# Twelve of thirty-two loop sums as three 16-bit products, and the projection moved ahead of the messages

## The reference

```python
h = x @ W_loop.T
g = h @ Wg_loop.T
vals = (h + b_loop) * sigmoid(g + bg_loop)
x1 = layernorm(x + relu(adj.T @ vals))          # first layer, per graph
out = layernorm(x1 + (adj @ x1) @ weight[0] + bias)   # second layer, per graph
```

## Time and profile before

| | |
|---|---|
| median of 3 runs | 158.79 us (158.68 to 159.75) |
| the profiled execution | 159.41 us, of which its span is 157.7 us |
| TensorE busy in that span | 148.8 us (94%) |
| VectorE, ScalarE, GpSimd busy | 124.1, 122.8, 125.7 us (79%, 78%, 80%) |
| mean granted TensorE clock | 0.987 of full speed |

### The profile page before, as it was taken

One profiled execution on the slowest core, in us unless ns is written; L12 is line 12 of the kernel. 1 busy time (PEld: TensorE's weight loads), 2 busy tenths in 40 slices (PEclk: granted clock), 3 DMA queues, 4 the chain that ended last, 5 costly groups with the idle time before them and its releaser, 6 DMA issues.

```text
span 157.7 us, 3520 instructions
## 1 busy us (share of the span) xinstructions
PE 148.8 (94%) x1040; PEld 136.7 (87%) x1040; DVE 124.1 (79%) x325; ACT 122.8 (78%) x255; POOL 125.7 (80%) x195
## 2 busy tenths in 40 slices
PE   7999999999999999999999999999999999999910
PEld 3688999999999999999999999999999999999800
DVE  1359988888988888887988888887888878989980
ACT  3357876979797997979797997979797997769850
POOL 0606698797979799797979799797979799797970
PEclk9999999999999999999999999999999999999995
DMA  4899999989797988979797989989693929211053
GB/s 126 292 405 394 370 389 404 390 265 389 198 382 230 331 303 258 354 241 398 177 392 209 356 290 286 340 237 373 192 393 130 381 92 303 86 69 69 4 201 138
DMA packets 19606, 42.73 MB, mean 271 GB/s; under 512 B 2177, under 2 KB 3073, under 8 KB 19585
## 3 DMA queue, kind: packets, MB, share of 16 engines
q1 hardware_dynamic: 14544, 25.76, 48.6%
q0 software_dynamic: 4752, 16.52, 30.3%
q10 hardware_dynamic: 288, 0.20, 0.4%
HBM read 34.08 MB, written 8.39 MB: 269 GB/s over the span
## 4 chain that ended last, share of the span: by engine, by line
POOL 65%; PE 15%; issue 13%; DVE 1%; POOLq 1%; ACT 0%; DVEq 0%
POOL rstd L339 31%; POOL x L353 26%; PE hg_ps L423 7%; POOL adj_sb L326 4%; POOL adjt_sb L333 3%; PE loop_ps L439 2%; PE msg_ps L458 2%; PE msg_ps L413 1%; PE y_ps L497 1%; PE hg_ps L407 1%; POOL rstd L363 1%; POOLq L59 1%; DVE s_sb L808 0%; ACT gate L607 0%; POOLq L234 0%
## 5 line engine op out<-in xcount | busy, mean ns | idle before, releaser
L339 POOL TENSOR_TENSOR rstd<-var,power 128x8 f32<-128x8 f32 (+1 forms) x36 | 53.8, 1496 | 18.5 <-DVE var L787 18.4
L423 PE MATMUL hg_ps<-w_all,xt_sb 128*128 128x256 f32 x256 | 65.7, 382 | 0.0
L353 POOL TENSOR_SCALAR x<-s_sb,mean_neg,rstd 128x128 f32<-128x128 f32 x120 | 52.2, 448 | 3.4
L423 PEld LDWEIGHTS hg_ps<-w_all,xt_sb 128*128 128x128 f32 x256 | 44.6, 193 | 4.1 <-issue 0.3
L626 ACT ACTIVATE out_sb<-z_sb,rstd 128x128 f32<-128x128 f32 x120 | 38.1, 390 | 0.4 <-POOL rstd L339 0.4
L800 DVE TENSOR_TENSOR vals<-hg_ps,gate 128x512 f32<-128x512 f32 x32 | 22.1, 690 | 19.3 <-ACT gate L607 19.3
L439 PEld LDWEIGHTS loop_ps<-vals,adj_sb 128*128 128x128 f32 x256 | 33.3, 191 | 1.9 <-issue 0.2
L598 ACT ACTIVATE hg_ps<-gate_b 128x1024 f32<-128x1024 f32 (+1 forms) x32 | 31.8, 998 | 3.2 <-DVE vals L800 2.6
L458 PEld LDWEIGHTS msg_ps<-adjt_sb,x 128*128 128x128 f32 x248 | 31.4, 191 | 3.1 <-issue 1.5
L439 PE MATMUL loop_ps<-vals,adj_sb 128*128 128x128 f32 x256 | 33.8, 275 | 0.1
L458 PE MATMUL msg_ps<-adjt_sb,x 128*128 128x128 f32 x248 | 33.2, 277 | 0.0
(11 more groups left out here) (64 smaller groups left out, 48.2 us busy)
## 6 DMA issues: line engine op xcount, KB each, us to landing
xt_sb<-x_t_dram SPq DMA_DIRECT2D x32, 256.0 KB, 4.9
x_sb<-x_dram SPq DMA_DIRECT2D x32, 256.0 KB, 4.2
out<-out_sb SPq DMA_DIRECT2D x31, 256.0 KB, 4.7
adj_sb<-adj_dram POOLq DMA_DIRECT2D x15, 512.0 KB, 5.2
adjt_sb<-adj_t_dram POOLq DMA_DIRECT2D x15, 512.0 KB, 6.5
adjt_sb<-adj_t_dram POOLq DMA_DIRECT2D x2, 256.0 KB, 6.7
first_edges<-adj_dram SPq DMA_DIRECT2D x1, 256.0 KB, 4.2
adj_sb<-adj_dram POOLq DMA_DIRECT2D x1, 256.0 KB, 6.3
```

What stands on the lines that cost most here:

```text
L339: nc.gpsimd.tensor_tensor(rstd[:, c % RSTD_RING, first:end, :].rearrange("p l b -> p (l b)"), var[:, c % 2, first:end, :].rearrange("p l b ...
L353: done = nc.gpsimd.tensor_scalar(x1[:, q % X1_RING, batch(b)], s_sb[:, q % S_RING, batch(b)], mean_neg[:, c % 2, b:b + 1], rstd[:, c % RST ...
L423: last = nc.tensor.matmul(hg_ps[:, q % 2, b, :], xt_sb[:, q % XT_RING, batch(b)], w_gate, start=False, stop=True, skip_group_check=True)
```

## The change

The loop sums of the groups 5, 7, ... 27 (`SPLIT`, twelve of them) are no longer one fp32 product per graph. VectorE cuts the values into three bf16 parts that add up to the fp32 number: the upper half of the fp32 word as it stands, the upper half of what is left (`below`), and the rest (`lowest`). TensorE multiplies each of the three with the adjacency, which for these groups lies in SBUF as bf16, and adds them up in PSUM. So that a DMA fills a tile of one type, the pairs of groups are loaded as two even groups (fp32) and two odd groups (bf16) from group 4 to group 27 (`unit_of`, `unit_end`).

Beside it: the projection of a group runs in one piece, ahead of the messages; ScalarE computes the gate ahead of the copy of messages; the copy of negated means is gone, and those who read it subtract the mean instead; two of the five bf16 products on the constant tile just ahead of the loop are gone; the next-to-last group is scaled by ScalarE and stored from ScalarE's queue.

```diff
+SPLIT = tuple(range(5, GROUPS - 4, 2))
...
+def unit_of(q):
+    j = q // 4
+    return (2 * j + q % 2, q % 4 // 2) if 4 <= q < GROUPS - 4 else (q // 2, q % 2)
+def unit_end(k):
+    return 4 * (k // 2) + 2 + k % 2 if 2 <= k < PAIRS - 2 else 2 * k + 1
...
             def load_adj(k):
-                    await_count(pool, loop_done, 2 * (k - ADJ_RING) + 2)
-                    pool.dma_start(adj_sb[:, 2 * spot:2 * spot + 2, :].rearrange("p g n -> p (g n)"), adj[k])\
+                        pool.wait_ge(loop_done, unit_end(k - ADJ_RING) + 1)
+                    edges = adj_sb[:, 2 * spot:2 * spot + 2, :]
+                    source = adj[k].rearrange("p (g n) -> p g n", g=2)
+                    if 2 <= k < PAIRS - 2:
+                        if k % 2 == 1:
+                            edges = half_edges(spot)
+                        first = k // 2 * 2
+                        source = adj[first:first + 2, :, k % 2 * W:(k % 2 + 1) * W].rearrange("g p n -> p g n")
+                    pool.dma_start(edges, source).then_inc(adj_in[spot], 16)
...
-            for _ in range(5):
+            for _ in range(3):
                 nc.tensor.matmul(msg_ps[:, :], warm[:, :], warm_wide, start=True, stop=True)
...
             def loop_sum(q):
+                    if q in SPLIT:
+                        pe.wait_ge(split_done, SPLIT.index(q) + 1)
                     for b in range(GB):
+                        if q in SPLIT:
+                            edges = half_edges(unit % ADJ_RING)[:, place, batch(b)]
+                            nc.tensor.matmul(loop_ps[:, batch(b)], edges, upper_half(vals[:, q % 2, batch(b)]),
+                                             start=True, stop=False)
+                            nc.tensor.matmul(loop_ps[:, batch(b)], edges, upper_half(below[:, batch(b)]),
+                                             start=False, stop=False)
+                            last = nc.tensor.matmul(loop_ps[:, batch(b)], edges, lowest[:, batch(b)],
+                                                    start=False, stop=True)
...
-                else:
-                    messages(t - MSG_LAG)
                 project(t, (2, 3))
+                messages(t - MSG_LAG)
...
+                gates(t)
                 copy_messages(t - MSG_LAG)
-                gates(t)
...
+            norm2(GROUPS - 2, every)
+            act.wait_ge(out_done, GROUPS - 1)
+            act.dma_start(out[GROUPS - 2], out_sb[:, (GROUPS - 2) % OUT_RING, :])\
...
+            def split(q):
+                await_count(dve, loop_done, q - 1)
+                dve.wait_ge(vals_done, q + 1)
+                tt(below[:, :], vals[:, q % 2, :], upper_half(vals[:, q % 2, :]), ALU.subtract).then_inc(below_done, 1)
+                dve.wait_ge(below_done, SPLIT.index(q) + 1)
+                tt(lowest[:, :], below[:, :], upper_half(below[:, :]), ALU.subtract).then_inc(split_done, 1)
...
                 values(t)
+                if t in SPLIT:
+                    split(t)
                 first_sum(t - LOOP_LAG)
...
-            last_norm2(LAST - 1, 0, GB, root_count(GROUPS + 2, 1))
```

More of the change, by code:

```diff
@@ L77, in build @@
         vals = sb("vals", [P, 2, W], F32)
+        below = sb("below", [P, W], F32)
+        lowest = sb("lowest", [P, W], BF16)
         s_sb = sb("s_sb", [P, S_RING, W], F32)
@@ L224, in build, with mean_of, upper_half, half_edges @@
         warm_wide = warm[:, None, :].broadcast_to([P, GB, P])
+        def mean_of(c, b):
+            return stats[:, c % STATS_RING, b // 2, 3 * (b % 2) + 1:3 * (b % 2) + 2]
         def batch(b):
             return slice(b * P, (b + 1) * P)
+        def upper_half(tile):
+            return tile.bitcast(BF16).rearrange("p (n two) -> p n two", two=2)[:, :, 1]
+        def half_edges(spot):
+            return adj_sb[:, 2 * spot:2 * spot + 2, :].rearrange("p g n -> p (g n)").bitcast(BF16)\
+                .rearrange("p (g n) -> p g n", g=2)[:, :, 0:W]
         def arrived(q, ring):
@@ L289, in _ @@
                 store(q)
[L290 to L291 removed]
             for p in range(2):
                 span = slice(2 * p * P, 2 * (p + 1) * P)
[L294 removed]
+                sp.wait_ge(out_dve, p + 1)
                 sp.dma_start(out[LAST, :, span], out_sb[:, LAST % OUT_RING, span])\
@@ L354, in norm1 @@
                         x1[:, q % X1_RING, batch(b)], s_sb[:, q % S_RING, batch(b)],
-                        mean_neg[:, c % 2, b:b + 1], rstd[:, c % RSTD_RING, 0, b:b + 1], ALU.add, ALU.mult)
+                        mean_of(c, b), rstd[:, c % RSTD_RING, 0, b:b + 1], ALU.subtract, ALU.mult)
                 done.then_inc(x1_done, 1)
@@ L429, in loop_sum @@
                 if exists(q):
-                    spot = q // 2 % ADJ_RING * 2 + q % 2
+                    unit, place = unit_of(q)
+                    spot = unit % ADJ_RING * 2 + place
                     if q == 0:
@@ L433, in loop_sum @@
                     else:
-                        pe.wait_ge(adj_in[q // 2 % ADJ_RING], arrived(q // 2, ADJ_RING))
+                        pe.wait_ge(adj_in[unit % ADJ_RING], arrived(unit, ADJ_RING))
                     pe.wait_ge(vals_done, q + 1)
+                    if q in SPLIT:
+                        pe.wait_ge(split_done, SPLIT.index(q) + 1)
                     await_count(pe, s_done, q)
                     for b in range(GB):
-                        last = nc.tensor.matmul(loop_ps[:, batch(b)], adj_sb[:, spot, batch(b)],
-                                                vals[:, q % 2, batch(b)], start=True, stop=True)
+                        if q in SPLIT:
[6 more added lines that the diff above has]
+                                                    start=False, stop=True)
+                        else:
+                            last = nc.tensor.matmul(loop_ps[:, batch(b)], adj_sb[:, spot, batch(b)],
+                                                    vals[:, q % 2, batch(b)], start=True, stop=True)
                     last.then_inc(loop_done, 1)
@@ L660, in look @@
                     await_count(act, seen_done, k)
-                    nc.scalar.activation(seen[:, :], adj_sb[:, 2 * spot:2 * spot + 2, :].rearrange("p g n -> p (g n)"),
+                    edges = adj_sb[:, 2 * spot:2 * spot + 2, :]
+                    if 2 <= k < PAIRS - 2 and k % 2 == 1:
+                        edges = half_edges(spot)
+                    nc.scalar.activation(seen[:, :].rearrange("p (g n) -> p g n", g=2), edges,
                                          ACT.Square, bias=half[:, 0:1],
@@ L783, in variances @@
                 both = stats[:, c % STATS_RING, 2 * first:2 * end, :].rearrange("p c (i k) -> p (c i) k", k=3)
-                if first == 0:
-                    await_count(dve, x1_done, c - 2)
-                    ts(mean_neg[:, c % 2, :], both[:, 0:GB, 1], -1.0, None, ALU.mult)
                 ts(var[:, c % 2, first:end, :].rearrange("p l b -> p (l b)"), both[:, :, 2], 1.0 / P, EPS,
```

16 lines of the change are left out of this document (9 added, 7 removed).

## The result

The changed kernel takes 191.49 us (median of 4 runs, 190.77 to 193.79), the kernel before in the same session 159.27 (4 runs): 1.2005 times as long, with a 95% interval of 1.1908 to 1.2102. That is far above the predicted range. The profiled execution has a span of 192.1 us and a granted TensorE clock of 0.989 (before 0.987), so the clock plays no part. It is the longest of the four runs and left out of the ratio; 1.5 us of it is a wait ahead of the first projection, which the other kernels with the same start don't show.

What follows compares the result with a forecast made beforehand. TensorE was taken to set the pace before, the loop through GpSimd and ScalarE after: +1.4 us for the loop, -0.3 start, -0.4 tail, so +0.7 and a median from 158.79 to 159.5 us; range 156.5 to 163.2.

Steps and rivals of the forecast that it cites:

- The copy of means gives back 0.08.: VectorE's time: dropping the copy of negated means saves 0.08 us, part of its 8.80 us per pair of steps.
- GpSimd's norm instructions keep their length: Sign to look for in the changed profile: GpSimd's norm no longer than before, root and norm together 3.41 us.
- 0 to 0.05: TensorE's wait for ScalarE's copy of messages, in steps whose loop sum isn't split and takes 0.90 us.
- 8.73 to 8.93: Microseconds TensorE by itself needs per pair of steps, with split products and the waits for ScalarE's copy.
- The split on TensorE: Loop sum of split groups: twelve bf16 products at 0.056 us each, 0.67 in all, 0.22 us less per pair.
- The rival of slow products: Split products take 0.11 us each, 9.25 us per pair, 163.3 us in all; chance 0.10 together with longer DMA issues.
- 0.13 to 0.28: TensorE's wait in microseconds for ScalarE's copy of messages, in steps whose loop sum is split and takes 0.67.
- The loop: Chain VectorE, GpSimd, ScalarE, message weights decides: 8.91 to 8.99 us per pair, taken as 8.94, +1.4 us over twelve pairs.
- if that doubled: GpSimd's first load issue, 0.59 us, taken at its old price; doubled by smaller pieces, a pair would take 9.24 us.
- Subtractions against GpSimd: Rival: VectorE's two-SBUF-input subtractions and GpSimd's norm block each other, loop +0.43 to 0.86 us, 162.1 to 164.7 us; chance 0.20.
- Late adjacency: Rival: odd groups' adjacency lands too late for the loop sum, 0.3 us per pair, +3.6, 163.1 us; chance 0.05.
- The ends: Start with two products fewer, -0.3 us (0 to -0.6); tail with the store on ScalarE's queue, -0.4 (-1.1 to +0.3).

Runs made afterwards that it cites:

- e2: Kernel before, with GpSimd's norm subtracting the mean read from the statistics instead of adding the negated copy: 189.72 us, ratio 1.1924.
- e3: Kernel before, with the copy of means not negated and all its readers, GpSimd's norm included, subtracting it: 189.43 us, ratio 1.1903.
- e4: Kernel before, with the means negated in place in the statistics' tile and GpSimd's norm adding them from there: 159.51 us, ratio 1.0007.
- e11: Kernel before, with GpSimd's norm as multiply, then subtract (not the norm proper, the mean being unscaled): 190.31 us, ratio 1.1928.
- e12: Kernel before, with GpSimd's norm as multiply, then add (again not the norm proper): 159.18 us, ratio 0.9986.
- e1: Changed kernel, with VectorE's negated copy of the means back and GpSimd's norm adding it: 165.32 us, ratio 1.0388.
- e7: e1 with no group split, all loop sums and adjacency in fp32; new grouping, order and ends stay: 162.32 us, ratio 1.0203.
- e9: e1 with adjacency loaded one pair of steps earlier and one operand of each VectorE subtraction from PSUM (not a true split): 162.86 us, ratio 1.021.
- e6: e1 with every adjacency load issued one pair of steps earlier: 164.04 us, ratio 1.0292.
- e5: e1 with one operand of each new VectorE subtraction read from PSUM, which leaves out the split itself: 164.92 us, ratio 1.0344.

## Why the prediction was wrong

**The step that failed** is in the part on VectorE: "The copy of means gives back 0.08." I priced the removal of the copy and gave no price at all to those who had read it. GpSimd's norm was carried on at 3.41 us for root and norm, and "GpSimd's norm instructions keep their length" stands among the signs as if it needed no reason. They grew from 448 to 796 ns: 4 x 0.348 = 1.39 us per group, 2.78 per pair, on an engine with 0.8 to spare. With 0.2 more for each first load, that gives 8.06 + 2.78 + 0.2 = 11.04 us, and 11.09 was measured. The 2.27 us over 8.82, some fifteen times, make 34 us; the span grew by 34.4, of which 1.5 is the wait at the start. e2 gives the loss by that edit alone, e3, e4, e11 and e12 show that it is the subtraction on GpSimd, and e1 gives 26 us back by undoing it. None of my rivals held it: the one that touched GpSimd had it disturbed by VectorE, never its own instruction changed. The kernel before has no subtraction on GpSimd, so its trace had no price for one, and its cost should have been bounded from both sides. With 0.8 us to spare and eight norm instructions in a pair, 0.1 us more for each would have been the point from which GpSimd decides.

**The rest of the change** would have been slower too, 3.9% (e1), where I forecast 0.4%. By ratios of the chain of experiments, on 159.4 us: 3.2 us are there without the split (e7; the ends' gain of 0.6 is in it, so order, handover and the new grouping of loads cost about 3.8), 0.1 come with split products once contention and late loads are away (e9 less e7), 1.3 are contention (e6 less e9) and 1.5 late adjacency (e1 less e6). Each of these has an uncertainty of about a microsecond. The 0.1 is a balance and not the price of the loop: in e9's profile TensorE's pairs lose 0.30 us to the wait for the copy five times and 0.09 once, 1.6 us in all, while e7 has its one late load (0.65) and a start that is 0.34 us later.

*TensorE in the new order.* Waits of "0 to 0.05" for the unsplit loop sum were right: 0.05. What I left out is the 0.07 us by which a group that starts after a wait is longer; its row stood there, 1.13 us for the message weights of the start beside 1.06 in the steady step, and I used it for the handover only. With 0.12 on each step TensorE needs 9.06 for an unsplit pair, and not "8.73 to 8.93" with the split. Pairs with a split group take just as much (9.05 in e9), so the faster products give TensorE nothing. The mean step before was 4.42 and not 4.41, as the messages of one step in four took 0.94 us (72.28 to 73.22); 26 steps ran in the new order, and 26 x 0.11 makes 2.9 us, which with e7's late load is most of the 3.8.

*The split on TensorE.* Twelve products, 0.057 us apart, 0.69 in all, where I took 0.056 and 0.67: right. The pace that I halved, 0.43 us for 512 columns, stands in a stretch with a granted clock of 1.00, so that the products would be twice as fast in the loop was assumed and not read; 0.057 bears it out. The rival of slow products falls. What they win goes into the wait for the copy, as predicted: in the changed kernel the last product's turn ends at 90.91 and message weights start at 91.17, 0.26 us later, within "0.13 to 0.28".

*VectorE.* In e9 values start 2.55 us after the odd step's projection (2.56 predicted), the subtractions at 3.35 and 4.07 (3.29 and 4.02), the sum at 4.68 (4.62). In the changed kernel the subtractions take 693 and 691 ns, against 0.69. Right.

*The loop.* In e9 GpSimd's root starts at 84.24 - 77.72 = 6.52 (6.38), the next root ends at 12.95 (12.57), look at 15.11 (14.69), message weights at 17.45 (16.93 to 17.08). They are 0.37 late or more, 0.14 from VectorE's side and 0.19 from the DMA issues (1.33 instead of 1.14), and their group takes 0.96: two pairs in 18.41 us, a mean of 9.20 and not 8.94. The mechanism was right, its size too small by 0.26. In the changed kernel it doesn't show, as GpSimd's own work is longer than any loop through it.

*The DMA issue.* 0.59 became 0.75 to 0.80; "if that doubled" was the end of the range, the old price the value taken, and the truth lay between.

*Subtractions against GpSimd.* Priced at 0.43 to 0.86 us for the loop with a chance of 0.20. In e1 norm grows by 0.44 to 0.98 in a split step, and with one operand in PSUM (e5) it doesn't. This agrees with the rule cited from the Trainium skill, page "SBUF — State Buffer", section "Who interferes with whom", that two SBUF inputs are what contends; how long the one blocks the other, no run here tells. The rival is real, but at 1.2 to 1.3 us of time and not at 4.0 to 6.6: the longer norm stands behind the loop's last root, and only the 0.13 us that VectorE's second subtraction loses is in the loop (e6 and e9). In the changed kernel the two rarely meet, since GpSimd is so late that the subtractions fall on its root: one starts at 95.48, the other at 96.21, and norm at 97.13 only.

```profile
95.48 0.69 DVE L849 TENSOR_TENSOR below<-vals 128x512 f32<-128x512 f32 x1
96.21 0.69 DVE L851 TENSOR_TENSOR lowest<-below 128x512 bf16<-128x512 f32 x1
```

*Late adjacency.* A chance of 0.05 was too small. In e1 the loads take 6.9 us in the middle where the kernel before had 5.4, and my 1.2 us to spare were worked out with the old landing time. Why they land later there is open. The same grouping all in fp32 has 5.4 (e7), so it isn't the smaller pieces alone; without the contention it is 6.7 (e5), so it isn't that; and the slower changed kernel, bf16 tiles and all, has 5.3.

*The ends.* -0.57 us together, -0.7 predicted. But it is all at the start, where I took -0.3, and nothing at the tail, where I took -0.4: that the sum came so near is luck.

## What to carry to other kernels

When a change drops a small instruction, price its readers, not only the instruction: each operand or operation that changes in them is a new instruction, to be measured by itself where the trace has none of its kind, first of all on an engine with less than a tenth to spare. Here adding a negated mean costs VectorE under 0.1 us per group and saves GpSimd 1.4. A handover that takes 0.8 to 0.95 us needs more than 0.9 us of other work between its two sides, since meeting it exactly already costs, and a gain on the bound engine is worth no more than the slack of the loop through all the others.

## What the runs showed of the hardware

- GpSimd's instruction with two per-partition scalars on 128x128 fp32 takes 0.45 us as add and multiply, in either order (448, 453, 454 ns), and 0.79 us as soon as one of the two is a subtraction, also in either place (794, 794, 797 ns). On VectorE the same exchange costs nothing: 376 ns with the subtraction (e3), 374 before.
- Two VectorE subtractions of 512 columns with both inputs in SBUF lengthen four GpSimd norm instructions from 1.73 us to between 2.17 and 2.71, and the second of them takes 691 to 824 ns itself (e1); with one input in PSUM the norm keeps its length (e5).
- GpSimd takes 0.75 to 0.80 us to issue a load of 256 pieces of 2 KB, and 0.59 to 0.63 for 128 pieces of 4 KB with the same bytes.
- A bf16 product of 128 columns with a fresh weight follows the one before it by 0.057 us, and a group of eight fp32 products that starts after a wait takes 0.96 to 0.97 us to the next group's start instead of 0.89.
